# Fourth layer: the last 16 node tiles as two groups of 8, the first turned to nodes in the third layer's last units

## The reference, cut to what matters

```
# layer 2 (the third): log map between all pairs, weighted, then the exp map
log_ij = _logmap(x[:, None, :], x[None, :, :], c)
agg = jnp.einsum('ij,ijc->ic', adj / deg, log_ij)
x = x + _expmap(origin, agg @ weight + bias, c)
# layer 3 (the fourth)
h = jnp.maximum(_layernorm(x, axis=-1), 0.0)
support = h @ weight
mask = (adj != 0)
rank = cumsum(mask, axis=1);  deg = rank[:, -1:];  k = minimum(deg, 100)
pos = rank - (deg - k)
w = mask * where(pos > 0, 0.5 ** (k - pos), 0.0)
x = x + w @ support + bias
```

## Time and profile before

| | |
|---|---|
| median of 3 runs (range) | 1047.3 us (1044.82 to 1051.48) |
| profiled execution, its own time | 1044.31 us |
| its span, first to last instruction | 1042.6 us |
| mean granted TensorE clock | 0.981 |
| TensorE busy | 980.6 us (94%) |
| VectorE busy | 850.0 us (82%) |
| ScalarE busy | 750.8 us (72%) |
| GpSimd busy | 298.0 us (29%) |
| third layer's last unit, pair value | 951.46 us after the start |
| fourth layer's steps | about 953 to 1036 us |

### The profile page before, as it was taken

One profiled execution on the slowest core, in us unless ns is written; L12 is line 12 of the kernel. 1 busy time (PEld: TensorE's weight loads), 2 busy tenths in 40 slices (PEclk: granted clock), 3 DMA queues, 4 the chain that ended last, 5 costly groups with the idle time before them and its releaser, 6 DMA issues.

```text
span 1042.6 us, 16458 instructions
## 1 busy us (share of the span) xinstructions
PE 980.6 (94%) x6171; PEld 475.1 (46%) x6171; DVE 850.0 (82%) x1080; ACT 750.8 (72%) x805; POOL 298.0 (29%) x140
## 2 busy tenths in 40 slices
PE   6999979999899999999989999999999999998888
PEld 2444444446644444435434444444455454333455
DVE  6999969998678676697769987878878978888883
ACT  4655545554477667686788989988888888997683
POOL 1069980000001000004015464434343444342001
PEclk9999989999989999999998999999999999999999
DMA  9989987994048899788753444555655553446662
GB/s 330 420 332 422 423 366 241 345 403 162 1 160 282 292 304 301 262 268 303 261 188 127 160 127 158 170 194 164 198 163 162 165 171 116 155 142 201 214 217 78
DMA packets 96350, 238.43 MB, mean 229 GB/s; under 512 B 16401, under 2 KB 45073, under 8 KB 79889
## 3 DMA queue, kind: packets, MB, share of 16 engines
q1 hardware_dynamic: 87056, 220.62, 61.5%
q10 hardware_dynamic: 9216, 16.78, 4.2%
HBM read 219.55 MB, written 17.83 MB: 228 GB/s over the span
## 4 chain that ended last, share of the span: by engine, by line
PE 62%; DVE 20%; ACT 9%; issue 7%; POOL 1%; DMA 1%; DVEq 0%; SPq 0%; ACTq 0%; POOLq 0%
PE PS L577 39%; PE PS L756 9%; DVE TB L1559 6%; PE PS L896 4%; PE PS L865 4%; DVE work L2078 2%; ACT work L1268 2%; ACT work L1276 2%; DVE work L2066 2%; DVE ring L2084 1%; ACT work L1279 1%; DVE work L2072 1%; PE PS L589 1%; DVE work L1729 1%; ACT work L1262 1%
## 5 line engine op out<-in xcount | busy, mean ns | idle before, releaser
L555 POOL TENSOR_TENSOR ring<-work,ring 128x1024 f32<-128x1024 f32 x57 | 135.3, 2374 | 232.8 <-DVE work L2078 232.7
L1729 DVE TENSOR_TENSOR work<-work,ring 128x1024 f32<-128x1024 f32 x128 | 152.9, 1234 | 58.0 <-ACT work L1193 57.9
L1193 ACT ACTIVATE work<-PS,att_sc 128x1024 f32<-128x1024 f32 x128 | 148.0, 1201 | 68.5 <-PE PS L756 59.5
L1118 ACT ACTIVATE work<-PS 128x1024 uint8<-128x1024 f32 x128 | 124.2, 1024 | 100.0 <-PE PS L577 99.9
L577 PE MATMUL PS<-ring,work 128*65 128x256 f32 (+1 forms) x600 | 190.4, 465 | 3.8 <-DVE work L2105 3.8
L577 PE MATMUL PS<-work 128*64 128x512 f32 (+2 forms) x800 | 151.5, 519 | 1.4 <-ACT work L1262 1.2
L2072 DVE SCALAR_TENSOR_TENSOR work<-PS,work 128x1024 f32<-128x1024 f32 x72 | 88.0, 1222 | 55.0 <-PE PS L577 46.5
L756 PE MATMUL PS<-work 128*64 128x512 f16 x1024 | 124.0, 384 | 3.0 <-ACT work L1193 1.6
L577 PEld LDWEIGHTS PS<-ring,work 128*65 128x65 f32 x600 | 80.6, 138 | 90.7 <-issue 65.5
L1268 ACT ACTIVATE work<-work 128x1024 f32<-128x1024 f32 x72 | 76.0, 1055 | 34.8 <-DVE work L2066 34.7
L756 PEld LDWEIGHTS PS<-work 128*64 128x64 f16 x1024 | 59.0, 111 | 79.4 <-issue 34.7
(11 more groups left out here) (280 smaller groups left out, 1402.1 us busy)
## 6 DMA issues: line engine op xcount, KB each, us to landing
ring<-in_adj_t SPq DMA_DIRECT2D x96, 1024.0 KB, 5.4
ring<-in_adj_t SPq DMA_DIRECT2D x104, 512.0 KB, 4.1
work<-in_adj_t SPq DMA_DIRECT2D x32, 1024.0 KB, 8.6
codes<-work ACTq DMA_DIRECT2D x64, 256.0 KB, 7.2
ring<-codes SPq DMA_DIRECT2D x64, 256.0 KB, 4.6
H<-in_adj_t SPq DMA_DIRECT2D x24, 512.0 KB, 4.2
X<-in_x SPq DMA_DIRECT2D x2, 256.0 KB, 5.2
X<-in_x SPq DMA_DIRECT2D x1, 512.0 KB, 10.4
```

Of the source, the lines that this page charges most:

```text
L555: nc.gpsimd.tensor_tensor(near(n), sums(n), near(n), ALU.mult).then_inc(sem("near_ready"), 1)
L1118: nc.scalar.activation(made[:, k, u:HALF:2], PS[:, (4 + 2 * u) * BANK:(6 + 2 * u) * BANK], ACT.Relu).then_inc(sem("codes_made"), 1)
L1193: nc.scalar.activation(att[:, u, :], PS[:, (4 + 2 * u) * BANK:(6 + 2 * u) * BANK], ACT.Sigmoid, bias=att_sc[:, 2:3], scale=att_sc[:, 1:2]) ...
L1729: V.tensor_tensor(prob[:, m % 4, :], att[:, u, :], ring[:, s % RING, u * UNIT:(u + 1) * UNIT], ALU.mult)\
```

## The change

GROUPS has four groups of 8 tiles. The order of the 64 steps changes with it: tiles 16 to 23 in both halves are steps 32 to 47, tiles 24 to 31 steps 48 to 63, and half 0 is complete at step 55. Group 2's nodes are made on TensorE after unit 69's gathers and copied out by ScalarE after unit 70's roots; VectorE does its tangent_dot and tangent_scale after the sum of unit 71. Its remaining parts, and all of group 3, stand at new places in last_passage3 of the three engines. tangent_part, tangent_own and tangent_sum of group 2 come on VectorE right after power 1, and to_tangent(2) on TensorE ahead of step 1. Group 3 is turned to nodes ahead of step 5; its to_tangent is ahead of step 10 on TensorE, and its tangent_sum ahead of power 13 on VectorE. The banks and the semaphore counts are adapted. ScalarE copies half 0 after all its powers, and TensorE turns it to nodes ahead of step 60. No operation on data is added or taken away, but those over 16 tiles become two over 8.

```diff
@@ -75,14 +75,17 @@
 AUX_R, AUX_L = 13, 14
 
 
-GROUPS = ((0, 8), (8, 16), (16, 32))
+GROUPS = ((0, 8), (8, 16), (16, 24), (24, 32))
 
 
 PIECES = ((24, 32), (16, 24), (0, 16))
-COMPLETE = (36, 52, 72)
-COPIES = (2, 4, 7)
+COMPLETE = (36, 52, 66, 72)
+COPIES = (2, 4, 6, 8)
+LAST_BANK = (1, 3, 2, 3)
 VISITS = {38: ("agg2_copied", 2), 41: ("turned_out", 1), 42: ("z_out", 1), 51: ("turned_out", 2), 52: ("z_out", 2),
-          54: ("agg2_copied", 4), 57: ("turned_out", 3), 58: ("z_out", 3)}
+          54: ("agg2_copied", 4), 57: ("turned_out", 3), 58: ("z_out", 3), 69: ("agg2_copied", 6)}
+TANGENTS = (1, 3, 4, 6)
+LASTS = (2, 5, 7, 8)
 CAUGHT = 16
 TANH_TOP = 7.90531110763549805
 TANH_NUM = (-2.76076847742355e-16, 2.00018790482477e-13, -8.60467152213735e-11, 5.12229709037114e-08,
@@ -314,7 +317,7 @@
         def linear_out(q, last=False):
 
             a, b = GROUPS[q]
-            bank = (1, 3 if last else 1, 2)[q]
+            bank = LAST_BANK[q] if last else 1
             return PS[:, bank * BANK:bank * BANK + (b - a) * D].rearrange("p (t c) -> p t c", c=D)
 
         adj_tiles = adj_t.rearrange("(t p) n -> t p n", p=P)
@@ -905,7 +908,7 @@
 
             def through(q, w, b_row):
                 a, b = GROUPS[q]
-                bank = (1, 3 if b_row is None else 1, 2)[q]
+                bank = LAST_BANK[q] if b_row is None else 1
                 for u in range((b - a) // 2):
                     if u % 4 == 0 and b_row is not None:
                         bias_rows(b_row, bank + u // 4)
@@ -918,15 +921,15 @@
                 turn(q, cen)
 
             def weighted(q):
-                pe.wait_ge(sem("turned_out"), 2 * q + 1)
+                pe.wait_ge(sem("turned_out"), TANGENTS[q])
                 through(q, wbd["w2"][:, :], 4)
 
             def to_last(q):
                 pe.wait_ge(sem("feats_ready_l3"), q + 1)
-                turn(q, cen, 3 if q == 1 else 0)
+                turn(q, cen, LAST_BANK[q] if q else 0)
 
             def weighted_last(q):
-                pe.wait_ge(sem("turned_out"), 2 * q + 2)
+                pe.wait_ge(sem("turned_out"), LASTS[q])
                 pe.wait_ge(sem("w3_done"), 2)
                 through(q, wbd["w3"][:, :], None)
 
@@ -953,6 +956,8 @@
                     to_tangent(1)
                 if n == 58:
                     weighted(1)
+                if n == 69:
+                    nodes2(2)
 
             def gather2_near(n):
                 S, p = UNITS[n]
@@ -1032,26 +1037,36 @@
 
             def last_passage3(q):
 
+                if q == 1:
+                    pe.wait_ge(sem("agg2_copied"), COPIES[2])
+                    to_tangent(2)
                 if q == 2:
                     gather2_near(NU - 1)
                 if q == 3:
+                    weighted(2)
+                if q == 4:
                     pe.wait_ge(sem("far_out"), mirrors(NU - 1))
-                    nodes2(2)
-                if q == 4:
                     to_last(1)
+                if q == 5:
+                    pe.wait_ge(sem("z_out"), TANGENTS[2])
+                    nodes2(3)
                 if q == 6:
                     weighted_last(1)
-                if q == 8:
-                    pe.wait_ge(sem("agg2_copied"), COPIES[2])
-                    to_tangent(2)
                 if q == 10:
-                    pe.wait_ge(sem("z_out"), 4)
-                    weighted(2)
-                if q == 25:
+                    pe.wait_ge(sem("agg2_copied"), COPIES[3])
+                    to_tangent(3)
+                if q == 12:
+                    weighted(3)
+                if q == 19:
                     to_last(2)
-                if q == 27:
+                if q == 21:
                     weighted_last(2)
-                if q == 52:
+                if q == 32:
+                    pe.wait_ge(sem("z_out"), LASTS[1])
+                    to_last(3)
+                if q == 34:
+                    weighted_last(3)
+                if q == 60:
                     pe.wait_ge(sem("sums_out3_a"), 1)
                     to_nodes(ident[:, :], 0, 0).then_inc(sem("agg3_nodes"), 1)
 
@@ -1307,6 +1322,9 @@
             def part_a(q, k):
                 one("part_a", S3(*GROUPS[q], 0), part(cen, q), ACT.Copy, ("z_out", k))
 
+            def last_a(q, k):
+                one("part_a", S3(*GROUPS[q], 0), linear_out(q, True), ACT.Copy, ("through", k))
+
             def root_part(name, wait, before, q):
                 act.wait_ge(sem(wait), before + 1)
                 nc.scalar.activation(part(st[2], q), part(st[1], q), ACT.Ln).then_inc(sem("act_chain"), 1)
@@ -1343,6 +1361,8 @@
                     v_square(1, 3)
                 if n == 61:
                     root_part("v_root", "v_norm2", 1, 1)
+                if n == 70:
+                    nodes2_out(2)
 
             square2(0)
             for n in range(NU):
@@ -1358,31 +1378,41 @@
                     ln_square(1)
                 if q == 3:
                     root_part("ln_sd", "ln_var", 3 * G + 1 + 1, 1)
+                if q == 4:
+                    turned_out(2, 4)
+                if q == 5:
+                    z_out(2, 4)
+                    v_square(2, 4)
                 if q == 7:
-                    nodes2_out(2)
+                    turned_out(1, 5, 3)
                 if q == 8:
-                    turned_out(1, 4, 3)
-                if q == 10:
-                    z_out(1, 4, last=True)
-                    part_a(1, 4)
-                if q == 13:
-                    turned_out(2, 5)
-                if q == 15:
-                    z_out(2, 5)
-                    v_square(2, 5)
+                    nodes2_out(3)
+                    root_part("v_root", "v_norm2", 2, 2)
+                if q == 9:
+                    z_out(1, 5, last=True)
+                    part_a(1, 5)
+                if q == 12:
+                    turned_out(3, 6)
+                if q == 14:
+                    z_out(3, 6)
+                    v_square(3, 6)
+                    ln_square(2)
+                if q == 16:
+                    root_part("ln_sd", "ln_var", 3 * G + 1 + 2, 2)
                 if q == 19:
-                    root_part("v_root", "v_norm2", 2, 2)
-                if q == 26:
-                    ln_square(2)
+                    root_part("v_root", "v_norm2", 3, 3)
+                if q == 22:
+                    turned_out(2, 7, 2)
+                if q == 24:
+                    last_a(2, 7)
+                if q == 25:
+                    ln_square(3)
                 if q == 28:
-                    root_part("ln_sd", "ln_var", 3 * G + 1 + 2, 2)
-                if q == 29:
-                    turned_out(2, 6)
-                if q == 30:
-                    one("part_a", S3(*GROUPS[2], 0), linear_out(2), ACT.Copy, ("through", 6))
-                if q == 56:
-                    one("sums_out3_a", TA[:, 0:UNIT], PS[:, 4 * BANK:6 * BANK], ACT.Copy, ("agg3_done", 48),
-                        scale=W_SCALE / (F16_TOP / LN_TOP))
+                    root_part("ln_sd", "ln_var", 3 * G + 1 + 3, 3)
+                if q == 36:
+                    turned_out(3, 8, 3)
+                if q == 38:
+                    last_a(3, 8)
 
             def power(q):
                 act.wait_ge(sem(code_loaded(q)[0]), code_loaded(q)[1])
@@ -1402,6 +1432,8 @@
             for q in range(2 * T):
                 last_passage3(q)
                 power(q)
+            one("sums_out3_a", TA[:, 0:UNIT], PS[:, 4 * BANK:6 * BANK], ACT.Copy, ("agg3_done", 56),
+                scale=W_SCALE / (F16_TOP / LN_TOP))
             one("sums_out3_a", TA[:, UNIT:UNIT + BANK], banks(6, 7), ACT.Copy, ("agg3_done", 2 * T),
                 scale=W_SCALE / (F16_TOP / LN_TOP))
 
@@ -2045,6 +2077,9 @@
                     mean3(1)
                 if n == 69:
                     centre3(1)
+                if n == 71:
+                    tangent_dot(2)
+                    tangent_scale(2)
 
             def power(q):
                 dve.wait_ge(sem(code_loaded(q)[0]), code_loaded(q)[1])
@@ -2129,41 +2164,69 @@
             dve.wait_ge(sem(f"near_loaded{n % RING2}"), 16 * (n // RING2 + 1))
             V.tensor_tensor(near(n), sums(n), near(n), ALU.mult).then_inc(sem("last_near"), 1)
             power(1)
+            tangent_part(2)
+            tangent_own(2)
+            tangent_sum(2)
+            power(2)
             spread3(1)
-            power(2)
+            power(3)
             feats3(1)
-            power(3)
             near2_out(n)
 
+            def last_rest(q):
+                dve.wait_ge(sem("part_a"), q + 1)
+                V.tensor_tensor(S3(*GROUPS[q], 1), linear_out(q, True), S3(*GROUPS[q], 0), ALU.subtract)\
+                 .then_inc(sem("parts3_ready"), 1)
+
             def last_passage3(q):
-                if q == 10:
-                    tangent_dot(2)
-                    tangent_scale(2)
-                    tangent_part(2)
-                    tangent_own(2)
```

(51 more changed lines are left out.)

## The result

The changed kernel takes a median of 1051.69 us (20 runs, 1045.48 to 1059.89) against 1047.26 us for the kernel before (20 runs, 1044.77 to 1052.21). The ratio is 1.0044, with an interval of 1.0027 to 1.0062: 4.4 us slower, less than 1%. The forecast was 1052.5. The profiled execution of after has a span of 1051.1 us and a time of 1052.86 at a mean granted clock of 0.984.

A forecast was written before the change was run, and what follows sets the result against it. TensorE, busy 94% of the span, sets the end; what can be won lies in its waits for VectorE and ScalarE. +3.1 us at full clock and +2.1 for low clock make +5.2 on 1047.3: 1052.5 us, range 1046 to 1058.

The forecast's parts named there:

- The nodes' 1.84 us: TensorE, unit 69: the moved nodes find no gap, so unit 71's scores and unit 70's sides come 1.84 us later.
- Dot and scale in the third layer: VectorE, unit 71: 1.82 us of new work between sum and pair, the pair coming 3.3 us later.
- The first gap: TensorE after step 0: idles 4.0 us in front of to_tangent(2), until VectorE finishes group 2's tangent at 959.8.
- The wait at step 10: TensorE waits 4.8 us for group 3's tangent; VectorE's work from v_root to it takes 8.9 us.
- The price of the split on VectorE: Splitting the 16-tile group doubles the tiny operations and gives VectorE about 6 us more work.
- The small waits and the end: TensorE begins step 25 at 1000.3, does not stop after step 32, and ends the last step at 1038.2.
- The clock: Low clock after the two gaps adds +2.1 us: the first stretch's 1.5 in full, half of the second's 1.2.
- (b): Rival, chance 0.22: the third layer's end finds cover for the new work; +1.9, or about 0 without low clock.
- (c): Rival, chance 0.08: faster; TensorE's waits at 987 to 1003 go and none takes their place, 1039.8.
- (d): Rival, chance 0.10: slower by over 1%; low clock after both gaps and at steps 21 to 25, 1054.6 or, with mishaps, past 1057.8.

The follow-up runs named there:

- before_nodes: Kernel before, with the 16 node matmuls of tiles 16 to 23 made once more after unit 69's gathers, result unread: 1047.86 us, ratio 1.0012.
- near_first: Changed kernel, with the adding of the near sums and power 0 moved ahead of group 2's dot and scale on VectorE in unit 71: 1055.1 us, ratio 1.0082.
- nodes_at_71: Changed kernel, with group 2's nodes after unit 71's work and its dot and scale behind the last product and power 1: 1054.05 us, ratio 1.0072.
- after_busy: Changed kernel, with 18 matmuls of constants before the last layer's first gather and 18 before step 10's tangent wait: 1049.56 us, ratio 1.002.
- after_fewer: Changed kernel without nine tiny tanh operations in each of groups 2 and 3, so node values differ: 1047.97 us, ratio 1.0009.
- before_fewer: Kernel before without nine tiny tanh operations for its 16-tile group, so node values differ: 1047.18 us, ratio 0.9996.
- plan: Groups of 8 kept as in the changed kernel, every piece of the passages placed elsewhere in the three queues: 1040.51 us, ratio 0.9931.
- late_only: Changed kernel up to step 9 on TensorE, with plan's order only for what follows: 1042.88 us, ratio 0.994.
- early_only: Changed kernel with plan's order only up to step 9; it also moves group 2's tanh numerator behind v_root: 1050.43 us, ratio 1.0019.

## Why the prediction was right, and where one step was off

The time, the sign and the mechanism held, but that 1052.5 came within 0.8 us of 1051.69 is partly luck, as two of the terms show. Point by point, in distances from the ruler's start:

**The nodes' 1.84 us.** Held: 1.82 (944.68 to 946.50). The sum of unit 71 moved by 1.74; I had said 1.6. before_nodes shows the cause by itself.

**Dot and scale in the third layer.** I had 3.3 us for the pair; it moved from 8.41 to 12.25, that is 3.84. Most of the excess, 0.36, is in one operation: the dot took 1.04 us where its like takes 0.68. So the last product came later than I had it, by 0.5.

**The first gap: this step failed, though its sum held.** I wrote that TensorE idles 4.0 us after step 0, ahead of the turn of group 2. It idled 0.85 there, and 4.66 us ahead of the gather of unit 70, 5.5 in all where there had been 2.53. I had priced the adding of the near sums (0.60) as an item between dot and pair and did not ask who waits for it, though the earlier trace rows named it, L2105, as what ended that very gap. near_first and nodes_at_71 show that the two places share one budget: with less in the first there is more in the second (2.45 and 3.07; 0.80 and 2.89), because the tangent, at 17.3 us (16.75 forecast), comes at its own time. It is why this mistake cost no accuracy. That is luck. What it could have cost is a wrong edit: near_first is just the one that it suggests, and it wins nothing.

**The wait at step 10.** 4.8 forecast, 4.51 measured, with the turn at 37.7 instead of 36.45: of the 1.3, 1.1 is there when v_root is done (973.31, 28.6 behind the start; forecast 27.55), half of it the 0.5 above, the rest small items of TensorE's work between the two tangents. The chain from v_root to tangent_sum took the 8.9 us of the forecast. after_busy (the place doesn't move when the low clock ahead of the first tangent goes) and after_fewer (it moves when VectorE has less to do) show that the chain is on the path; near_first shows that TensorE's work between the two tangents is too. The price of the split on VectorE was right as well: about 6 us more work forecast, 6.2 on the ruler (73.29 us busy against 67.09).

**The small waits and the end.** Steps 24 to 27 start at 1004.73, 60.05 us behind the start, so step 25 at about 61.0; I had it at 1000.3, 57.25 behind. Of the 3.8 us between, 1.3 are the turn's and 2.3 the low clock behind it, which the walk to this place left out and the term of the clock holds. Steps after 32 don't stop, as said. From 1008.90 to the last turning are 36.0 us.

**The clock.** Forecast +2.1 us: the first low stretch in full, the second by half. after_busy gives 2.3 back by the ruler, but that is against all low clock, also the share that the kernel before has (two stretches of 3.4 us), so the net share of the change isn't isolated. The split was the wrong way round: the first stretch cost nothing, since VectorE set the next place anyway, and the second cost everything. That the term of 2.1 stands near 2.3 is luck. The Trainium skill ("TensorE: Matmul & The Clock Gate", "HAM oscillation") says that bursts between waits start cold. The trace of the change agrees at the gaps of 4.66 and 4.51 us, where the clock was low when TensorE went on. In near_first, behind 2.45 and 3.07 us, it fell only 1.2 and 0.7 us after TensorE had gone on, and behind the 2.53 us of the kernel before it didn't fall, while before_fewer has a low stretch 0.7 us behind the end of the same wait.

**The account.** The ruler's +6.9 is +4.2 of idle and +2.7 of busy time. Idle: first gaps +2.4 (5.5 less 2.53, 0.38 and 0.24), step 10 +4.5, small waits 3.4 instead of 6.0, -2.7. The moved nodes are no term of their own: the 32 of the kernel before, 3.76 us at 958.48, became 16 and 16, and their cost shows as later waits. Busy: 650 matmul records both times. The low clock, 10.2 us instead of 6.8, would make up to 1.7 of the 2.7; the rest, about 1, I can't place. The median's 4.4 is 2.5 below the ruler; one profile of each can't say how much of that is chance.

**The rivals.** (b) falls: before_nodes finds no cover for the nodes. (c) falls for the change, but the gain that it named, 1039.8, exists: plan reached 1040.51 by moving the same pieces. I had given the condition as tiny operations cheaper than 0.20 us; it was the places instead. (d) is outside the interval.

**Where the split's gain went.** The change took 2.7 us out of the waits at 987 to 1003 and handed back 6.9 in those ahead of them, because it called for group 2's tangent at step 1 and group 3's at step 10. Plan calls for them ahead of steps 4 and 15 and never waits over 0.93 us. late_only and early_only divide the 13.9 us of ruler between change and plan: 9.3 for the places from step 10 on, 2.2 for those ahead of it, 2.4 only when both are done. Of the last two, 1.4 belongs to the numerator's move in early_only, so by that estimate the places ahead of step 10 are worth 3.6, and 1 comes only when both are done.

## What to carry to other kernels

When one engine makes results ahead into a ring of buffers and another uses them up, the user feels a long block on the maker only when the ring is empty. So place such a block where the ring is full, and let the user ask for the block's result as late as its own use allows. That better order was worth 6 us here without any splitting, and splitting without it lost 4. When a piece is put into an in-order queue, list what stands behind it and who waits for each of those, not only who waits for the piece. Expect a shortened wait to pass to the next one in the same queue when both hang on one chain: in near_first 2.2 us went from the first to the second. And before a single profile is read for a gain, compare TensorE's busy time for the same matmuls: in before_fewer it was 3.6 us more than in the kernel before, which hid a gain of 1.26.
